# xDeepFM forward pass, one core: pair 0's rows sent straight to the engines, five copied tiles in pair 0 and a sixth copy for pair 1, pair 2's layout and fetch placed between the first copies

## The reference

```python
emb = tables[feat_idx, sparse]                     # 512 x 26 x 32
linear_out = lin_sparse_w[feat_idx, sparse].sum(-1) + dense @ lin_dense_w
x0 = emb; xk = emb; res = []
for w, bb in ((conv1_w, conv1_b), (conv2_w, conv2_b)):
    hp = einsum('bhd,bmd->bhmd', xk, x0).reshape(-1, h * M, E)
    xn = sigmoid(einsum('oi,bid->bod', w, hp) + bb)
    xk = xn[:, :half]; res.append(xn[:, half:])
cin_out = (concatenate(res, axis=1).sum(-1) @ cin_w + cin_b)[:, 0]
h1 = tanh(deep_x @ W1 + b1); h2 = tanh(h1 @ W2 + b2); h3 = tanh(h2 @ W3 + b3)
return linear_out + cin_out + (h3 @ deep_w + deep_b)[:, 0] + bias[0]
```

## Time and profile before

| | |
|---|---|
| Time, median of 3 runs | 415.51 us (414.73 to 419.06) |
| Time of the profiled execution | 415.48 us |
| Its span | 413.6 us |
| PE busy | 400.0 us (97%) |
| DVE busy | 311.5 us (75%) |
| Data moved | 74.14 MB |

### The profile page before, as it was taken

One profiled execution on the slowest core, in us unless ns is written; L12 is line 12 of the kernel. 1 busy time (PEld: TensorE's weight loads), 2 busy tenths in 40 slices (PEclk: granted clock), 3 DMA queues, 4 the chain that ended last, 5 costly groups with the idle time before them and its releaser, 6 DMA issues.

```text
span 413.6 us, 5230 instructions
## 1 busy us (share of the span) xinstructions
PE 400.0 (97%) x1854; PEld 167.1 (40%) x1854; DVE 311.5 (75%) x345; ACT 160.7 (39%) x267; POOL 169.6 (41%) x146
## 2 busy tenths in 40 slices
PE   3999979999999999999999999999999999999997
PEld 1432323333333333333333333333333335887885
DVE  4019579899898989898989889898989897442123
ACT  3074334544544544435353544544443601111012
POOL 6763572654856654826655700000000355780000
DMA  5249689999999999899999999999967760420000
GB/s 206 43 98 237 165 206 239 236 245 234 254 246 226 241 217 235 215 226 225 225 244 220 231 226 237 202 225 212 229 158 200 202 156 14 115 76 2 0 0 3
DMA packets 42177, 74.14 MB, mean 179 GB/s; under 512 B 20593, under 2 KB 23025, under 8 KB 42150
## 3 DMA queue, kind: packets, MB, share of 16 engines
q1 hardware_dynamic: 38566, 72.03, 71.4%
q0 software_dynamic: 3584, 1.76, 2.9%
HBM read 72.06 MB, written 1.71 MB: 178 GB/s over the span
## 4 chain that ended last, share of the span: by engine, by line
PE 84%; DMA 7%; POOL 4%; issue 2%; SPq 1%; DVE 1%; ACT 0%; DVEq 0%
PE conv L494 42%; PE conv L472 17%; PE conv L515 8%; PE ring L515 7%; PE ring L484 5%; POOL emb L395 4%; PE ring L454 4%; DMA emb<-in_table,rows 2%; DMA laid<-emb 1%; DMA copied<-laid 1%; DMA raw<-laid 1%; PE ring L530 1%; SPq L332 1%; DMA idx_sb<-in_idx 0%; DVE copied L835 0%
## 5 line engine op out<-in xcount | busy, mean ns | idle before, releaser
L395 POOL DMA_INDIRECT emb<-in_table,rows x112 | 137.2, 1225 | 98.0 <-DMA emb<-in_table,rows 66.3
L835 DVE TENSOR_TENSOR copied<-copied,xk 128x1024 f32<-128x1024 f32 x112 | 135.4, 1242 | 5.6 <-DMA copied<-laid 5.6
L835 DVE TENSOR_TENSOR prod<-ring,xk 128x1024 f32<-128x1024 f32 x96 | 113.9, 1214 | 31.3 <-ACT xk L661 30.8
L494 PE MATMUL conv<-copied,w_sb 128*64 128x512 f32 x448 | 105.5, 594 | 1.2 <-DVE copied L835 1.1
L494 PE MATMUL conv<-prod,w_sb 128*64 128x512 f32 x384 | 93.1, 605 | 0.9 <-DVE prod L835 0.9
L661 ACT ACTIVATE xk<-conv,const_sb 64x512 f32<-64x512 f32 x64 | 43.6, 682 | 124.7 <-PE conv L472 123.8
L472 PE MATMUL conv<-sq,w_sb 117*64 117x512 f32 x384 | 88.1, 593 | 0.3 <-ACT sq L690 0.3
L494 PEld LDWEIGHTS conv<-copied,w_sb 128*64 128x64 f32 x448 | 31.6, 137 | 65.4 <-issue 52.0
L650 ACT ACTIVATE sq<-ring 117x512 f32<-117x512 f32 x90 | 48.4, 596 | 4.7 <-PE ring L454 4.0
L404 POOL TENSOR_TENSOR xt_lo<-xt,xt_hi 128x512 fp32r<-128x512 f32 (+1 forms) x7 | 10.9, 1578 | 94.6 <-ACT xt_hi L727 90.0
L472 PEld LDWEIGHTS conv<-sq,w_sb 117*64 117x64 f32 x384 | 27.2, 136 | 54.2 <-issue 53.9
(11 more groups left out here) (97 smaller groups left out, 308.0 us busy)
## 6 DMA issues: line engine op xcount, KB each, us to landing
copied<-laid SPq DMA_DIRECT2D x224, 256.0 KB, 5.2
wpiece<-in_mlp SPq DMA_DIRECT2D x22, 256.0 KB
raw<-laid SPq DMA_DIRECT2D x64, 52.0 KB
emb<-in_table,rows POOLq DMA_INDIRECT x112
laid<-emb SPq DMA_DIRECT2D x16, 96.0 KB, 5.6
sel_f<-in_sel SPq DMA_DIRECT2D x1, 832.0 KB, 6.5
const_sb<-in_const SPq DMA_DIRECT2D x1, 626.5 KB, 4.7
w_sb<-in_w SPq DMA_DIRECT2D x1, 416.0 KB, 7.1
```

Source lines behind the costliest of these rows:

```text
L395: pool.indirect_dma_start(out=emb[0:n, i, j, :], out_offset=None, in_=table, in_offset=bass.IndirectOffsetOnAxis(ap=rows[0:n, i, j:j + 1], ...
L494: mm = nc.tensor.matmul(conv[i % 2][c * HALF:(c + 1) * HALF, :], w2_sb[:, t, :], prod_of(r)[:, c, :], start=(t == 0), stop=(t == T2 - 1))
L835: nc.vector.tensor_tensor(prod_of(r)[:, :, :].rearrange("p c n -> p (c n)"), left[:, :, :].rearrange("p c n -> p (c n)"), xk[i % 2][:, :, ...
```

## The change

It has these parts.

1. `DIRECT` is 1. Pair 0's rows go from `emb` into the buffer `copied5` by seven small transfers, each as soon as its gather has landed. ACT and DVE make x(0) from there, in two instructions each. Layout 0 stays, for the copies, and fetch 0 goes.
2. `WARM` is 9 instead of 12.
3. Pair 0 has five copied tiles (3, 6, 7, 8, 11) instead of seven, and so eight spread tiles. The sixth buffer, `copied5`, gets a tile of pair 1 once x(0) has been made. Helper functions that counted tiles by a formula look them up in lists now.
4. On SP, layout 2 stands after the fourth copy, then come the fifth copy, fetch 2 and the sixth copy.
5. On PE, pair 0's first three tiles are spread in one go; the two filler matmuls go to `conv[0]`; pair 0's last product is taken between the spreads of pair 1. On DVE, `x_low(2)` comes after tile 11 instead of tile 10.

```diff
--- before.py
+++ after.py
@@ -36,13 +36,12 @@
 DENSE_AT = 96
 RX = 3
 GSEM = 4
-DIRECT = 0
+DIRECT = 1
 XEND = HALF + XK
 RING = 3
 RP = 3
 COPIED = (2, 3, 6, 7, 8, 11, 12)
-SPREAD = tuple(t for t in range(T2) if t not in COPIED)
-NC, NS = len(COPIED), len(SPREAD)
+COPIED_0 = (3, 6, 7, 8, 11)
 RC = 6
 LAY_AT, FETCH_AT = 1, 4
 DEEP_IN = {0: (0, 1), 1: (2, 3), 2: (4, 5, 6)}
@@ -51,8 +50,8 @@
 SUMS_IN = {0: ((1, 2),), 1: ((2, 0),), 2: ((2, 1),)}
 L1_IN = {0: 0, 1: 1}
 X_LOW_1_AT = 1
-X_LOW_AT, TURN_AT, FOLD1_AT, PIECE_AT = (10, 5), 9, (5, 5), 11
-WARM = 12
+X_LOW_AT, TURN_AT, FOLD1_AT, PIECE_AT = (11, 5), 9, (5, 5), 11
+WARM = 9
 
 C_B1, C_B2, C_B3, C_DEEP, C_CB1, C_CB2, C_CIN1, C_CIN2, C_ONE, C_AUX, C_LOW, C_END = 0, 8, 12, 14, 16, 17, 18, 19, 20, 22, 23, 24
 SMALL_AT = 0
@@ -238,25 +237,30 @@
 
             return UT * c + u + 1 if i == 0 else 2 * (UT * i + u) + c + 1
 
+        copy_tiles = list(COPIED_0) + [T2 * i + t for i in range(1, NPAIR) for t in COPIED]
+        copy_number = {r: n for n, r in enumerate(copy_tiles)}
+        spread_tiles = [r for r in range(NTILE) if r not in copy_number]
+        spread_number = {r: n for n, r in enumerate(spread_tiles)}
+
         def spreads_up_to(r):
 
-            return NS * (r // T2) + SPREAD.index(r % T2) + 1
+            return spread_number[r] + 1
+
+        def spreads_of_pairs_up_to(i):
+
+            return sum(1 for r in spread_tiles if r < T2 * (i + 1))
 
         def copies_up_to(r):
 
-            return NC * (r // T2) + COPIED.index(r % T2) + 1
-
-        def tile_of_copy(n):
-
-            return T2 * (n // NC) + COPIED[n % NC]
-
-        def tile_of_spread(n):
-
-            return T2 * (n // NS) + SPREAD[n % NS]
+            return copy_number[r] + 1
+
+        def copies_of(i):
+
+            return [n for n, r in enumerate(copy_tiles) if r // T2 == i]
 
         def prod_of(r):
 
-            if r % T2 in COPIED:
+            if r in copy_number:
                 return copied[(copies_up_to(r) - 1) % RC]
             return prod[(spreads_up_to(r) - 1) % RP]
 
@@ -268,15 +272,17 @@
 
         for u in range(UT):
             enter(("sums", 0, u))
-        enter(("spread", SPREAD[0]))
-        enter(("spread", SPREAD[1]))
+        first = [r for r in spread_tiles if r < T2]
+        second = [r for r in spread_tiles if T2 <= r < 2 * T2]
+        for r in first[:3]:
+            enter(("spread", r))
         for u in range(UT):
             enter(("sums", 1, u))
-        for r in SPREAD[2:]:
+        for r in first[3:]:
             enter(("spread", r))
         for k in range(2):
             enter(("sums", 2, k))
-            enter(("spread", T2 + SPREAD[k]))
+            enter(("spread", second[k]))
         for i in range(1, NPAIR):
             for g in range(len(GROUPS)):
                 for j, u in sums_in(i, g):
@@ -334,10 +340,10 @@
 
             def copy(n):
 
-                r = tile_of_copy(n)
+                r = copy_tiles[n]
                 i, t = r // T2, r % T2
                 if n >= RC:
-                    sp.wait_ge(main_done, tile_of_copy(n - RC) + 1)
+                    sp.wait_ge(main_done, copy_tiles[n - RC] + 1)
                 sp.wait_ge(laid_in[i % RX], LAID * (i // RX + 1))
                 if RC - DIRECT <= n < RC:
                     sp.wait_ge(x_lo_done, n - (RC - DIRECT) + 1)
@@ -351,24 +357,25 @@
             sp.dma_start(w2_sb[:, :, :], w2).then_inc(w2_in, 16)
             sp.wait_ge(zeroed, 1)
             sp.dma_start(aux[DENSE_AT:DENSE_AT + ND, :], dense_t).then_inc(aux_in, 16)
+            direct(0)
             lay_out(0)
-            fetch(0)
             lay_out(1)
             fetch(1)
-            for n in range(RC):
+            for n in range(4):
                 copy(n)
             lay_out(2)
+            copy(4)
             fetch(2)
+            copy(5)
             sp.dma_start(xt[ML * E:K1_LAST, K1 - 1, :], dense_t).then_inc(dense_in, 16)
             for i in range(NPAIR):
                 if i < KW:
                     load_piece(i)
-                for k in range(NC):
-                    n = NC * i + RC + k
+                for k, n in enumerate(copies_of(i)):
                     if k == FETCH_AT and i + RX < NPAIR:
                         fetch(i + RX)
-                    if n < NC * NPAIR:
-                        copy(n)
+                    if n + RC < len(copy_tiles):
+                        copy(n + RC)
                     if k == LAY_AT and i + RX < NPAIR:
                         lay_out(i + RX)
             for k in range(KW, PIECES):
@@ -476,7 +483,7 @@
             def spread_tile(r):
 
                 i, t = r // T2, r % T2
-                if t == SPREAD[0]:
+                if t == 0:
                     pe.wait_ge(x_lo_done, i + 1)
                 slot_free("spread", r)
                 for c in range(2):
@@ -552,35 +559,35 @@
             pe.wait_ge(w1_step, 4)
             layer1(0, 0)
             pe.wait_ge(sel_done, 2)
-            spread_tile(SPREAD[0])
-            spread_tile(SPREAD[1])
+            for r in first[:3]:
+                spread_tile(r)
             layer1(0, 1)
             pe.wait_ge(w2_in, 16)
-            slot_free("sums", 1, 0)
+            pe.wait_ge(l1_read, 1)
             for k in range(2):
-                nc.tensor.matmul(sums_bank(1, 0)[:, 0, :], w2_sb[:, 0:2, :].rearrange("p t o -> p (t o)"),
+                nc.tensor.matmul(conv[0][:, :], w2_sb[:, 0:2, :].rearrange("p t o -> p (t o)"),
                                  w2_sb[:, 0:8, :].rearrange("p t o -> p (t o)"), start=True, stop=True)
             main(0)
             main(1)
             for u in range(UT):
                 sums_of(1, u)
             main(2)
-            spread_tile(SPREAD[2])
+            spread_tile(first[3])
             main(3)
-            spread_tile(SPREAD[3])
+            spread_tile(first[4])
             layer1(1, 0)
-            for r in SPREAD[4:-1]:
+            for r in first[5:]:
                 spread_tile(r)
             for t in range(4, 8):
                 main(t)
-            spread_tile(SPREAD[-1])
             layer1(1, 1)
             for t in range(8, T2 - 1):
                 main(t)
-            for k in range(2):
-                sums_of(2, k)
-                spread_tile(T2 + SPREAD[k])
+            sums_of(2, 0)
+            spread_tile(second[0])
             main(T2 - 1)
+            sums_of(2, 1)
+            spread_tile(second[1])
             for i in range(1, NPAIR):
                 for g, tiles_now in enumerate(GROUPS):
                     for j, u in sums_in(i, g):
@@ -637,7 +644,7 @@
                 if i < RX:
                     act.wait_ge(zeroed, 2 + i)
                 else:
-                    act.wait_ge(spread_done, NS * (i - RX + 1))
+                    act.wait_ge(spread_done, spreads_of_pairs_up_to(i - RX))
                 nc.scalar.activation(x[i % RX][0:XEND, :], raw[i % RX][0:XEND, :], ACT.Copy)\
                   .then_inc(x_hi_done, 1)
 
@@ -821,16 +828,16 @@
             for i in range(NPAIR):
                 for t in range(T2):
                     r = i * T2 + t
-                    n = copies_up_to(r) - 1 if t in COPIED else spreads_up_to(r) - 1
+                    n = copies_up_to(r) - 1 if r in copy_number else spreads_up_to(r) - 1
                     if t == 0:
                         dve.wait_ge(xk_ready, 4 * (i + 1))
-                    if t in COPIED:
+                    if r in copy_number:
                         dve.wait_ge(copy_in[n % RC], 32 * (n // RC + 1))
                         left = copied[n % RC]
                     else:
                         dve.wait_ge(spread_done, n + 1)
                         if n >= RP:
-                            dve.wait_ge(main_done, tile_of_spread(n - RP) + 1)
+                            dve.wait_ge(main_done, spread_tiles[n - RP] + 1)
                         left = spread_bank(r)
                     nc.vector.tensor_tensor(prod_of(r)[:, :, :].rearrange("p c n -> p (c n)"),
                                             left[:, :, :].rearrange("p c n -> p (c n)"),
```

## The result

| | before | changed |
|---|---|---|
| Time, median of 11 runs each | 415.53 us (413.98 to 419.06) | 420.59 us (419.10 to 421.67) |
| Profiled execution, time and span | 415.48, 413.6 us | 420.59, 418.8 us |
| Mean granted clock of TensorE | 1.000 | 0.988 |

The changed kernel takes 1.0112 times the time of before (95% interval 1.0093 to 1.0131): 5.1 us slower, and above the range of the prediction, 412.8 to 419.0 us.

The account below looks back on a forecast made before the run. PE alone counts from pair 3's first sum, which hangs on pair 3's gathers and x(3). With the landing left at 52.2 us, new idle time eats PE's head start, change 0: forecast 415.6 us, 8-in-10 range 412.8 to 419.0.

Parts of the forecast that it names:

- the place: PE's first sum of pair 3, at 63.97 us before; the end can move only as far as this instruction moves.
- its chain: Pair 3's gathers land, then layout 3, two copies, fetch 3 and x(3): 10.2 us from layout 3 to `x_high(3)`.
- So I leave the landing at 52.2.: Pair 3's last gather on POOL and layout 3 on SP: landing unchanged at 52.2 us, bounds 49.5 to 54.5.
- the same in number and size: Transfers beside pair 3's gathers: layout 2, two copies, fetch 2, a piece, two more copies, as before.
- the rival: Pair 3's rows meet more copies, so x(3) comes 2.3 us late: 417.9 us, chance 0.12.
- the sum: At pair 3's sums, 2 to 6 us of PE idle time eat the head start: change at the end 0, from -3.7 to +2.3.
- the rival at 1.3 to 1.9 us from the warm-up: PE's clock falls in the new idle time ahead of pair 3's sums, 1.3 to 1.9 us lost: 417.2 us, chance 0.30.
- The waits of PE may fill part of it: Argument against the clock rival: PE's waits may fill part of the new 2 to 6 us gap; no size given.
- The rival of both, 419.5 us: Pair 3's rows 2.3 us late and PE's clock falling too: 419.5 us; no separate chance given.
- the head start: PE can start pair 0's sums at 18.4 us, 3.0 us earlier, and reach pair 3's sums at 57.6 to 61.6.

Follow-up runs that it names:

- the pair of runs made for it: Kernel before, PE also waiting for pair 4's rows ahead of pair 3's first sum: idle 423.23 us; with five pairs of filler matmuls ahead of that wait 420.63 us.
- chips of the first kind: Runs on the two of four chips where the kernel before, unchanged, takes 415.6 and 415.7 us.
- the second kind: Runs on the other two chips, where the kernel before, unchanged, takes 421.5 to 422.9 us and traces show extra waits in the first 40 us.
- the first kernel with fillers: Changed kernel with 14 filler matmuls on PE ahead of pair 3's sums, first of three runs: 430.25 us, ratio 1.0177.
- the first with layout 3 ahead: Changed kernel with layout 3 ahead of copies 6 and 7 on SP, fetch 3 still behind four copies, first of three runs: 423.04 us, ratio 1.0015.
- the last version of the kernel before: Kernel before with layout 3 ahead of copies 6 and 7 and fetch 3 behind them: 419.06 us, ratio 1.0077.

## Why the prediction was wrong

**Right.** PE reached the place at 59.5 us (57.6 to 61.6 forecast), and pair 1's first product came at 50.0 (47.5 to 50). The part behind the first gap is filled without a gap. The place that counts and its chain were right.

**Less than forecast.** The sums of pair 0 started at 19.30 instead of 18.4, the first product at 28.46 instead of 27.6. `x_high(2)` came at 46.79, 0.8 us earlier than before instead of 3.3; fetch 2 stood between two copies, which is the likely reason. None of this decided.

**The step that failed: "So I leave the landing at 52.2."** It rested on counting the transfers beside pair 3's gathers, "the same in number and size". Their number is the same, their time is not. Before, the copies that precede layout 2 were issued by 34.7 us and then none until fetch 2 had gone; pair 3's gathers met two copies at their end, issued from 46.87 on. Now these two come 1.2 us earlier, from 45.68 on, and two more stand just ahead. Layout 3 went at 54.91 us in the changed kernel instead of 52.2. Over all traces it went at 51.4 to 54.9 us with the order of before (four), at 53.5 to 56.0 with the new one, and at 49.9 to 50.6 where copies 6 and 7 stand behind it (five, both orders). So these two copies beside the gathers make the landing late and uncertain; how much of the changed kernel's delay is the order and how much the draw, these few traces do not tell. The 52.2 that I took for a fixed point was one draw from 3.4 us of scatter, and an early one. In time the new order costs 1.9 us (0.9 to 2.4 by the 95% interval of the ratio). The Trainium skill (DMA: Bandwidth & Descriptors, queues, rings and completion order) says that each DMA engine takes turns between the queues that have work. The rows fit it: from the last gather's issue to layout 3 it took 1.4 to 2.7 us without copies 6 and 7 beside the gathers, 3.2 to 7.0 with them. They do not tell the number of the copies from their time. I had cited it for the rival and still gave that 0.12.

**The clock: right mechanism, wrong size, and left out of the sum.** The forecast had it at nothing, the rival at 1.3 to 1.9 us from the warm-up. Measured: 3.0 us in the changed kernel, 2.7 in the pair of runs made for it. The earlier trace rows show only the end of a slow time that may have begun earlier; a whole one, from the gap to the return, cost more in both cases. "The waits of PE may fill part of it" also failed: nothing stood in the gap. The Trainium skill (TensorE: Matmul & The Clock Gate, part 1) says that idleness brings the throttled state back, and the runs agree with 2.7 us.

**The sum.** The rival of both, 419.5 us, was the case that came true, with 2.5 us instead of 2.3 for the rows and 3.0 instead of 1.6 for the clock; the range stopped at 419.0, below this case. The mean clock was 0.988 to 0.992 in every one of the changed kernel's 11 runs, against 0.996 or 1.000 in all of before's that are on record from chips of the first kind, so the clock loss hardly depended on one late landing. The trace suggests why: PE arrives at 59.5, and with x(3) where the earlier trace rows have it the gap would still be 4.4 us, and each of the waits of 3.8 us or more listed at the end had the lower level behind it. The kernel before, with a landing as late, kept its clock. So the clock loss comes from the earlier arrival; no run took the head start alone, so this is argued from traces and not tested. The two parts then add up to 4.9 of the 5.1 us measured: 1.9 for the order, taken from the kernel before, and 3.0 for the clock. In the forecast's sum an earlier arrival at a fixed wait cost nothing; it was the larger loss.

## What to carry to other kernels

An engine that arrives earlier at a wait which doesn't move gains nothing, and PE can lose by it: give every new gap of PE the price of the lower clock behind it, measured from the gap to the return. Before moving large transfers in one queue, look at what the gathers of another queue are doing at that moment: the last gather's landing, not the count of transfers, sets what waits for it. A refill that is postponed in favour of a layout must be one that nobody needs yet.

## What the runs showed of the hardware

- PE gaps and the granted clock behind them. On chips of the first kind 6.89 us (twice) and 3.27 us were followed by matmuls at about half rate, eight on products in 3.68 or 3.29 us instead of 1.94; 2.79, 2.38, 2.33 and 2.31 us were not. On the second kind all nine gaps of 3.79 to 6.48 us (between 8 and 120 us) were followed by the lower level. But one of 3.56 us in the first kernel with fillers was not (clock 1.00), and one of 2.52 us, in the first with layout 3 ahead, was (0.56). So the length of the gap alone does not settle it. The level of 0.53 to 0.73 in the means is a mix of the two levels, 1.2 and 2.4 GHz.

```profile
56.80:63.40 6.60, 6.57 (x18) 2.10 (x20) 4.74 (x5) 2.81 (x5) 1.70 (x2) 0.53 1.05 229
```

(the stretch behind the gap of 3.27 us in the last version of the kernel before).

- The landing of seven gathers with copies beside them scatters by 3.4 us between executions of the same instructions (layout 3 at 51.44 to 54.85 us); without copies 6 and 7 beside them it came within 0.7 us (49.86 to 50.55), 1 to 5 us earlier.
- The kernel before took 6 to 7 us more on two chips than on two others, and the traces there show waits of up to 7 us in the first 40 us. So a comparison was only made on one chip, and the gap that decides on the first kind was hidden on the second.
- Gathers issued without a wait slowed everything to 1.28 times, at 27% of DMA busy time.

Open: what the direct rows, and the fewer copied tiles of pair 0, are worth alone on a chip of the first kind, and which of them gives the head start; what the extra waits of the second kind are; and what stops the engines when gathers run ahead.
